# Softmax denominators from sums of four probability tiles, one round of ones products a pair in place of two

## The reference

```python
q = (layer_norm(x) @ Wq); k, v = split(layer_norm(ctx) @ Wkv); k = apply_rope(k, cos, sin)
attn = clip(einsum('bhnd,bhsd->bhns', q, k) * 64**-0.5, -11, 11)
attn = softmax(attn, axis=-1)                 # sum over the 1024 context rows
x = x + einsum('bhns,bhsd->bhnd', attn, v) @ Wo + bo
sel = sigmoid(einsum('bsd,ed->bse', _layernorm(x), expert_sel))
x = x + einsum('bseh,ehv,bse->bsv', relu(_layernorm(x) @ keys), values, sel)
```

## Time and profile before

| | |
|---|---|
| median of 3 runs | 1156.72 us |
| the profiled execution | 1156.41 us, of which the span of instructions is 1154.6 us |
| PE busy | 1073.1 us (93%) |
| DVE busy | 813.0 us (70%) |
| ACT busy | 577.6 us (50%) |
| POOL busy | 381.8 us (33%) |
| mean granted TensorE clock | 0.982 |

### The profile page before, as it was taken

The page is one execution under the profiler, slowest core; times in us unless marked ns, Lnnn a source line. Parts: engine busy times, 40 slices in busy tenths (PEclk is TensorE's granted clock), DMA queues, the critical chain, the costliest instruction groups (busy, mean ns, idle before and its releaser), DMA issues. The chain is left out here.

```text
span 1154.6 us, 18383 instructions
## 1 busy us (share of the span) xinstructions
PE 1073.1 (93%) x5528; PEld 628.1 (54%) x5528; DVE 813.0 (70%) x1274; ACT 577.6 (50%) x909; POOL 381.8 (33%) x362
## 2 busy tenths in 40 slices
PE   3699998899999999999999999999999878999998
PEld 2454444455555555555555555555555436788886
DVE  6688778677777777777777777777777854554422
ACT  6665544455555555555555555555555532222221
POOL 6454333322222222222222222222222326545443
PEclk9899999899999999999999999999999988999999
DMA  5333322322222222222222222222222437223221
GB/s 142 116 105 109 89 82 74 107 71 71 82 81 74 71 71 71 71 78 74 88 89 71 71 71 71 71 76 83 78 71 65 125 100 264 80 91 128 92 110 37
DMA packets 67807, 103.13 MB, mean 89 GB/s; under 512 B 21952, under 2 KB 47488, under 8 KB 65728
## 3 DMA queue, kind: packets, MB, share of 16 engines
q1 hardware_dynamic: 67776, 102.75, 29.0%
HBM read 72.83 MB, written 10.75 MB: 72 GB/s over the span
## 5 line engine op out<-in xcount | busy, mean ns | idle before, releaser
L1163 DVE TENSOR_SCALAR probs<-probs 128x1024 f32<-128x1024 f32 x256 | 242.9, 973 | 189.1 <-ACT probs L968 189.0
L968 ACT ACTIVATE probs<-score_ps 128x1024 f32<-128x1024 f32 x256 | 248.9, 1025 | 244.7 <-PE score_ps L741 244.7
L758 PE MATMUL o_ps<-probs,v_sb 128*64 128x512 f32 x1024 | 252.9, 615 | 0.0
L1171 DVE TENSOR_TENSOR p_sum<-probs 128x1024 f32<-128x1024 f32 x128 | 158.5, 1238 | 5.8
L541 POOL TENSOR_TENSOR rstd_sb<-var_sb,power 128x2 f32<-128x2 f32 x40 | 38.5, 962 | 285.2 <-DVE var_sb L1107 285.2
L758 PEld LDWEIGHTS o_ps<-probs,v_sb 128*64 128x64 f32 x1024 | 63.1, 138 | 116.9 <-issue 85.6
L741 PE MATMUL score_ps<-q_hi,k_hi 64*128 64x512 f32 x512 | 115.1, 446 | 8.2 <-issue 8.2
L1480 POOL TENSOR_TENSOR act_lo<-act,act_hi 128x512 fp32r<-128x512 f32 x64 | 82.6, 1292 | 100.3 <-ACT act_hi L1628 100.3
L741 PEld LDWEIGHTS score_ps<-q_hi,k_hi 64*128 64x128 f32 x512 | 48.4, 185 | 120.0 <-issue 113.2
L566 POOL CAST wide_hi<-ctx_t 128x256 f32 (+1 forms) x30 | 29.4, 979 | 247.1 <-ACT x_t L928 247.1
L136 PE MATMUL job_ps<-wide_hi,w_hi 128*128 (+1 forms) x256 | 109.9, 429 | 1.1 <-POOL xT_lo L550 0.9
(11 more groups left out here) (175 smaller groups left out, 1858.1 us busy)
## 6 DMA issues: line engine op xcount, KB each, us to landing
k_swap<-k SPq DMA_DIRECT2D x128, 128.0 KB, 2.3
sel_all<-sel_dram SPq DMA_DIRECT2D x16, 1024.0 KB, 5.0
w_hi<-packs_hi SPq DMA_DIRECT2D x26, 512.0 KB, 3.5
w_lo<-packs_lo SPq DMA_DIRECT2D x26, 512.0 KB, 4.3
den<-inv_dram SPq DMA_DIRECT2D x64, 128.0 KB, 2.8
ctx_raw<-ctx SPq DMA_DIRECT2D x33, 128.0 KB, 2.1
packs_hi<-w_hi SPq DMA_DIRECT2D x8, 512.0 KB, 3.7
packs_lo<-w_lo SPq DMA_DIRECT2D x8, 512.0 KB, 4.5
```

The source lines that it names most:

```text
L758: mm = pe.matmul(o_ps[DH * h:DH * h + DH, :], v_sb[par][:, at:at + DH], probs[s % RING][:, h, :], start=(s == 0), stop=(s == STEPS - 1))
L968: act.activation(probs[s % RING][:], score_ps[s % 2][:], ACT.Exp, scale=DH ** -0.5).then_inc(exp_done, 1)
L1163: dve.tensor_scalar(probs[s % RING][:], probs[s % RING][:], CLIP_HI, CLIP_LO, ALU.min, ALU.max).then_inc(clipped, 1)
L1171: dve.tensor_tensor(p_sum[m][:], first, second, ALU.add).then_inc(summed_up, 1)
```

## The change

`sum_up` gets a second stage: after m = 1 and after m = 3, DVE adds the two `p_sum` tiles into a new tile `p_quad`, a sum of four probability tiles, behind a wait on its own `summed_up` (and one on `den_ready` of the pair before). `denominators` runs once a pair, where part 1 stood, from the two `p_quad` tiles; part 0, at the end of iteration n, goes. `p_sum` has two buffers in place of four, and ACT waits for one `den_ready` a pair.

```diff
-        p_sum = [sb(f"p_sum{i}", [P, 2, NQ]) for i in range(MACROS)]
+        p_sum = [sb(f"p_sum{i}", [P, 2, NQ]) for i in range(2)]
+        p_quad = [sb(f"p_quad{i}", [P, 2, NQ]) for i in range(2)]
...
-            def denominators(n, part):
-
-                wait(pe, summed_up, MACROS * n + 2 * part + 2)
-                if part == 0:
-
-                    wait(pe, den_evac, n)
-                    wait(pe, y_added, 2 * (n - 1))
+            def denominators(n):
+
+                wait(pe, quads_up, 2 * n + 2)
+                wait(pe, den_evac, n)
+                wait(pe, y_added, 2 * (n - 1))
                 for e in range(2):
                     for h in range(2):
                         at = DH * h + QUAD * e
-                        mm = pe.matmul(side_ps[at:at + QUAD, :], ones[:, 0:QUAD], p_sum[2 * part + e][:, h, :],
-                                       start=(part == 0), stop=(part == 1))
+                        mm = pe.matmul(side_ps[at:at + QUAD, :], ones[:, 0:QUAD], p_quad[e][:, h, :],
+                                       start=True, stop=True)
                 mm.then_inc(den_ready, 1)
...
                         attend(n - 1, STEPS - 1, nxt)
-                        denominators(n - 1, 1)
-                    if m == 3:
-                        denominators(n, 0)
+                        denominators(n - 1)
...
-            denominators(NPAIR - 1, 1)
+            denominators(NPAIR - 1)
...
-                wait(act, den_ready, 2 * n + 2)
+                wait(act, den_ready, n + 1)
...
                 wait(dve, clipped, STEPS * n + 2 * m + 2)
-                wait(dve, den_ready, 2 * n - 1 + m // 2)
+                wait(dve, quads_up, 2 * n + m // 2)
                 first, second = (probs[(2 * m + j) % RING][:] for j in range(2))
-                dve.tensor_tensor(p_sum[m][:], first, second, ALU.add).then_inc(summed_up, 1)
+                dve.tensor_tensor(p_sum[m % 2][:], first, second, ALU.add).then_inc(summed_up, 1)
+                if m % 2 == 1:
+
+                    wait(dve, summed_up, MACROS * n + m + 1)
+                    wait(dve, den_ready, n)
+                    dve.tensor_tensor(p_quad[m // 2][:], p_sum[0][:], p_sum[1][:], ALU.add).then_inc(quads_up, 1)
```

More of the change, by code:

```diff
@@ L352, in attention_phase @@
         summed_up = sem("summed_up")
+        quads_up = sem("quads_up")
         pv_done = sem("pv_done")
```

## The result

The changed kernel takes 1179.83 us, the median of four runs from 1178.36 to 1182.16, against 1156.79 us before (four runs, 1156.5 to 1157.69): the ratio of the times is 1.02, with a 95% interval from 1.0182 to 1.0218. It is slower by 23 us; the forecast was 1171.8, with a range of 1161 to 1188. The profiled execution took 1179.44 us, its span 1177.6 us.

The account below looks back on a forecast made before the run. Each pair was taken to be bound by DVE's chain in one stretch and PE in the other. The profiled 1156.4 us plus 11.8 gave 1168.2, the median 1168.5, with 3.3 for clock falls 1171.8 us; range 1161 to 1188.

Parts of the forecast that it names:

- A pair has two stretches, PE's and DVE's: In each pair, a PE saving counts only from project_y's second half to the next scores 2, a DVE addition only before.
- 1.00 us removed, +0.27 us a pair: Middle pairs: dropping part 0 saves PE 1.00 us, its wait for yT grows 1.27 us, net +0.27 us a pair.
- 1.27 us for the first addition, not 1.13: In m = 1 behind sum_up 1: DVE's chain grows by 1.27 us; by 1.13 if the dependence cost nothing.
- The addition in m = 3 costs nothing: Between sum_up 3 and scale_o: nearly all of DVE's idle 2.08 us is used, the price is nothing.
- Two falls of the clock in pairs 6 to 29: PE's clock at the wait of 1.97 us: two falls in 24 pairs, 3.3 us, from none to twelve.
- Pairs 0 and 1: 0.5 us: The first two pairs: 0.27 us for pair 1 and 0.2 for pair 0, where DVE has no idle time.
- Pairs 2 to 5: 2.0 us: Where POOL's work on weights holds DVE up: +0.5 us a pair, from 0 to 1, in all 2.0 us.
- The last two pairs: 2.8 us: Pairs 30 and 31: additions on DVE's chain with little or nothing to set against them, together 2.8 us.
- Many falls: Rival: the clock falls in a third or more of the pairs; twelve falls 1188 us, all 24 1208; chance 0.20.
- DVE did not become the bound: Rival: DVE becomes the bound everywhere; 0.5 us a pair lost at the pair's end gives 1184 us; chance 0.05.
- nothing hid in POOL's stall: Rival: the sum hides in DVE's stall behind POOL's product, saving 1.7 us a pair, 1116 us; chance 0.06.
- the time is no wash: Rival: the addition costs 1.0 to 1.1 us, the clock stays, the ends cancel, 1155 to 1159 us; chance 0.07.

Follow-up runs that it names:

- the round alone: The kernel before with the part 0 round of denominators taken out and no addition put in: 1122.69 us, ratio 0.9725.
- the additions alone: The kernel before with both rounds kept and DVE's two additions put in, their result unused: 1228.62 us, ratio 1.0634.
- the filled wait: The changed kernel with PE turning the context tile's blocks six times in place of once in pairs 4 to 29: 1168.34 us, ratio 1.0117.
- the first pairs spared: The changed kernel with the additions of pairs 0 and 1 made for 8 of 512 columns only: 1173.25 us, ratio 1.0148.
- the second addition alone: The kernel before with both rounds kept and only the addition of m = 3 put in, its result unused: 1157.49 us, ratio 1.0014.

## Why the prediction came out as it did

- *A pair has two stretches, PE's and DVE's.* Right, and shown from both sides: the round alone -1.0 us a pair with the wait unchanged, the additions alone +1.27 us with the round unchanged.
- *1.00 us removed, +0.27 us a pair.* Right: 26.2, 28.48 and 27.48 us for the three kernels, from 27.21.
- *1.27 us for the first addition, not 1.13.* Measured 1.25 (2.38 - 1.13). From sum_up 1 to the addition that waits for it takes 528.09 - 526.85 = 1.24 us, close to rope_add's 1.26; the statement of the Trainium skill ("VectorE: DVE Perf Modes", section "The DRAIN you can't avoid") that the semaphore costs nothing, which it measured on copies, doesn't hold for these additions either.
- *The addition in m = 3 costs nothing.* Right, 1157.5 us with it alone.
- *Two falls of the clock in pairs 6 to 29.* The term was sized 3.3 us; the profiled execution has four, 6.4 us. That PE's idling at this wait lets the clock fall is shown by the filled wait. That 1.9 us of idling is near the edge was right; the number was a guess from the waits' length, and length doesn't give it. The same wait led to 4 falls between pairs 6 and 29 in the changed kernel, 3 with the first pairs spared (247.90 to 276.95, 551.64 to 580.75 and 855.39 to 884.47 are the long pairs of that trace), 15 with both rounds kept. And the term counted these pairs only: pairs 0, 1 and 31 have falls besides, at places where the kernel before has none.
- *Pairs 0 and 1: 0.5 us.* This is the worst step: 5.7 us, and 6.2 counted from the first scores. I moved one operation and held the rest in place, where DVE had no idle time and shares access with POOL. The 0.2 us for pair 0 left out that the addition itself would wait 2 us for POOL's product, and that rope_add would then meet the next one; and neither pair's new waits were followed to the clock. Sparing the additions gives 5.9 us back.
- *Pairs 2 to 5: 2.0 us.* Measured 1.4. PE's wait for the addition to `yT` didn't grow there, since the added time came up one step earlier, at the turn of the context tile (1.31 to 1.47 us in place of 0.2).
- *The last two pairs: 2.8 us.* Measured 4.3. PE's wait for POOL in pair 31 is 3.41 us in place of 2.26, and at its end the clock falls, where it didn't before (0.54 in 935 to 942 us): from that wait's end to the end of the next long one takes 946.79 - 936.64 = 10.15 us in place of 924.13 - 916.68 = 7.45. That is the largest part, and the sum had no fall here. The denominators of pair 31 then wait 3.03 us for the second addition, which the sum hadn't followed either; the second addition alone already costs the end 2.9 us, where the sum had 1.2 for it.
- *The rivals.* None came true. Many falls asked for a third of the pairs and a pair in six had one; it came true in the additions alone, with two of three. DVE did not become the bound, nothing hid in POOL's stall, and the time is no wash.
- *How near the number is.* The forecast is 8 us low. The 1180 us at the upper end of its own range stood for seven falls; the 1179.8 measured are made of four, and of 5.7 us in pairs 0 and 1. That they meet is luck; the +0.27 us a pair is not.

What is left open: what decides in which pairs the clock falls (the changed kernel and the additions alone have the same waits, and differ in one round and in the pair's length, 27.48 and 28.48 us), and why executions reach their first scores anywhere from 49.0 to 51.2 us.

## What to carry to other kernels

Ask of a saving and of an addition not how busy their engines are but in which stretch they lie: here 1.00 us left the one stretch and 1.27 us came into the other, and the same addition 8 us later in the same loop (at 503.95 us, where its first place would have been at 495.70) cost nothing. An engine at 75% can be the one that is waited for; look for the wait that ends last, then for the idle time of the engine that ends it, and put new work directly ahead of that idle time. And where an engine waits for another in order, see whether work that waits for nothing stands behind the wait.

## What the runs showed of the hardware

Waits of 1.9 us on PE are enough for the granted clock to fall, at 1.6 us a time: in 3, 4 and 15 of the 23 intervals between pairs 6 and 29 of three kernels with the same waits. Ten transposes of 0.105 us in the wait stopped it. The Trainium skill ("TensorE: Matmul & The Clock Gate", section "HAM oscillation — how this bites in real kernels") expects no fall at gaps so short, and the runs differ. PE paid nothing for doing useless work while it waited, and here this gave most of 11.5 us.
